# Summing the gated squares over the channels: GpSimd adds the two halves first, TensorE multiplies once a group

## The reference

```
zxbcdt = rmsnorm(x) @ Win                      # z, xBC, dt
xBC    = silu(causal_conv(xBC)); xh, Bm, Cm = split(xBC)
y      = ssd(xh, dt, A, Bm, Cm) + reversed ssd + D * xh
y      = y * silu(z)                           # the gated y, 128 channels a token
y      = y * rsqrt(mean(y * y, -1) + 1e-6) * gn_w
x      = x + y @ Wout
```

## Time and profile before

| | |
|---|---|
| time, median of 3 runs | 2498.42 us (2494.3 to 2499.23) |
| span of the profiled execution | 2496.4 us |
| PE busy | 1980.1 us, 79% |
| DVE busy | 1670.7 us, 67% |
| ACT busy | 1666.6 us, 67% |
| POOL busy | 1090.7 us, 44% |
| first `sum_squares` of a block to the last in the program | 941.4 to 2470.5 us |

### The profile page before, as it was taken

How to read it: one execution, slowest core, us unless ns; L and a number is a source line. 1 busy time by engine, 2 the same in 40 slices (tenths; PEclk the granted TensorE clock), 3 DMA queues, 4 the chain that set the end, 5 groups by cost and what they waited for, 6 DMA issues and landing times.

```text
span 2496.4 us, 58563 instructions
## 1 busy us (share of the span) xinstructions
PE 1980.1 (79%) x24262; PEld 1001.1 (40%) x24262; DVE 1670.7 (67%) x2423; ACT 1666.6 (67%) x2731; POOL 1090.7 (44%) x858
## 2 busy tenths in 40 slices
PE   4367677776777679979979979967997997996996
PEld 3122222222222235535525535534553552553553
DVE  3488888888888766556656656656655765665663
ACT  1276677676676657757857857866775775785784
POOL 0044444444444525516606625623551660662563
PEclk6578888888988889989989989988988998998997
DMA  4000000000000021022012111102102201211111
GB/s 159 0 0 1 1 0 0 1 1 0 1 1 0 0 65 38 18 65 49 19 56 47 30 55 39 39 18 62 41 14 66 49 18 56 47 30 42 40 39 35
DMA packets 95513, 77.46 MB, mean 31 GB/s; under 512 B 65936, under 2 KB 74128, under 8 KB 94736
## 3 DMA queue, kind: packets, MB, share of 16 engines
q1 hardware_dynamic: 91984, 73.32, 11.7%
q10 hardware_dynamic: 3264, 0.39, 0.1%
HBM read 27.02 MB, written 11.53 MB: 15 GB/s over the span
## 4 chain that ended last, share of the span: by engine, by line
PE 55%; DVE 20%; ACT 15%; issue 6%; POOL 2%; DMA 1%; ACTq 0%; POOLq 0%; SPq 0%; DVEq 0%
PE bank L593 10%; PE bank L662 7%; PE bank L625 6%; PE bank L674 6%; PE bank L606 5%; PE bank L682 5%; DVE Z L1271 4%; PE bank L521 3%; ACT bank L935 3%; PE bank L577 2%; ACT Z L827 2%; DVE XP L1337 2%; ACT SS L832 2%; DVE bank L1263 2%; POOL Y L986 2%
## 5 line engine op out<-in xcount | busy, mean ns | idle before, releaser
L986 POOL TENSOR_TENSOR Y<-Z 128x512 f32<-128x512 f32 x256 | 330.6, 1292 | 496.9 <-DVE Z L1271 320.4
L1018 POOL TENSOR_TENSOR SQ<-SQ,folded_weights 128x512 f32<-128x512 f32 x192 | 243.8, 1272 | 676.0 <-DVE SQ L1448 675.9
L1271 DVE TENSOR_TENSOR_SCAN Z<-SS,bank 128x512 f32<-128x512 f32 x256 | 309.9, 1211 | 0.5
L521 PE MATMUL bank<-Y,constants 128*128 128x512 f32 x512 | 298.0, 668 | 7.7 <-DVE bank L1279 7.6
L1024 POOL TENSOR_TENSOR SQ<-O,SQ 128x512 f32<-128x512 f32 x208 | 264.8, 1274 | 64.9 <-ACT O L931 36.5
L593 PE MATMUL bank<-folded_weights,work 128*64 128x128 f32 x4096 | 287.2, 285 | 0.0
L625 PE MATMUL bank<-SS,work 32*128 32x512 bf16 x1024 | 209.7, 389 | 63.0 <-ACT bank L935 45.0
L662 PE MATMUL bank<-SQ,work 128*32 128x64 f32 x8192 | 259.1, 227 | 0.6
L593 PEld LDWEIGHTS bank<-folded_weights,work 128*64 128x64 f32 x4096 | 225.9, 140 | 79.0 <-issue 79.0
L509 PE MATMUL bank<-work,Z 96*128 96x512 bf16 x256 | 113.8, 445 | 175.1 <-DVE Z L1271 175.0
L1390 DVE SCALAR_TENSOR_TENSOR work<-SQ,bank 64x512 f32<-64x512 f32 x256 | 175.5, 685 | 108.7 <-ACT SQ L903 106.6
(11 more groups left out here) (264 smaller groups left out, 3757.5 us busy)
## 6 DMA issues: line engine op xcount, KB each, us to landing
work<-XP SPq DMA_DIRECT2D x256, 134.0 KB, 2.4
decays_kept<-extra SPq DMA_DIRECT2D x24, 384.0 KB, 2.3
SS<-decays_kept SPq DMA_DIRECT2D x256, 24.0 KB
block_weights<-callw SPq DMA_DIRECT2D x8, 735.0 KB, 4.3
work<-decays_kept SPq DMA_DIRECT2D x240, 24.0 KB
Z<-state_sel SPq DMA_DIRECT2D x1, 2048.0 KB, 13.2
out<-O SPq DMA_DIRECT2D x2, 1024.0 KB, 8.5
constants<-consts SPq DMA_DIRECT2D x1, 1451.5 KB, 6.3
```

The source lines that it names most:

```text
L521: mm(bank[7], ident, hc[ta % 4], start=(ta % S1 == 0), stop=(ta % S1 == S1 - 1), skip_group_check=True).then_inc(sg("s1_acc"), 1)
L986: g.tensor_tensor(hc[t_ % 4], hs[t_ % 4], c_copy[t_ % 4], ALU.mult).then_inc(sg("s1_hc"), 1)
L1018: g.tensor_tensor(MM[u % 3], MM[u % 3], Dhalf, ALU.add).then_inc(sg("mixed"), 1)
L1271: v.tensor_tensor_scan(hs[t_ % 4], decay1[t_ % 2], bank[B_BANKS[t_ % 3]], 0.0, ALU.mult, ALU.add).then_inc(sg("s1_h"), 1)
```

## The change

GpSimd gets a step of its own in each group, `add_squares(k)`: it waits for the two squares of ACT and adds `squares[1]` onto `squares[0]`. PE's `sum_squares` waits for that step instead of for ACT, and does one matmul on `squares[0]` instead of two. Where the step stands in GpSimd's loop: before the mixing of u = 15, 23, ..., 63 for groups 0 to 6, and behind the loop for group 7.

```
                 def sum_squares(g):
-                    pe.wait_ge(sg("gated_squared"), c * 8 + g + 1)
+                    pe.wait_ge(sg("squares_added"), c * 8 + g + 1)
                     pe.wait_ge(sg("z_ready"), c * 16 + min(2 * g + 4, 16))
                     if g >= 1:
                         pe.wait_ge(sg("scaled"), c * 8 + g)
-                    for hd in range(2):
-                        last = mm(bank[sum_bank(g)], C("ssum"), squares[hd], start=(hd == 0), stop=(hd == 1))
-                    last.then_inc(sg("squares_psum"), 1)
+                    mm(bank[sum_bank(g)], C("ssum"), squares[0], start=True, stop=True).then_inc(sg("squares_psum"), 1)
...
+                def add_squares(k):
+                    pool.wait_ge(sg("gated_squared"), c * 8 + k + 1)
+                    g.tensor_tensor(squares[0], squares[0], squares[1], ALU.add).then_inc(sg("squares_added"), 1)
+
                 for u in range(L):
+                    if u >= 15 and (u - 15) % 8 == 0:
+                        add_squares((u - 15) // 8)
                     if u >= 20 and (u - 20) % 8 == 0:
                         grow((u - 20) // 8)
...
+                add_squares(7)
                 grow(6)
                 grow(7)
```

## The result

The changed kernel takes 2503.22 us (median of 20 runs, 2498.53 to 2506.06), the kernel before 2498.61 us in the 20 runs beside it. The ratio is 1.0015, with a 95% interval of 1.0009 to 1.0022: 3.7 us slower by the ratio, 4.6 by the medians. The forecast was 2502.4. In what follows the time of a variant is the median of its runs, to be held against 2498.61 and 2503.22; the ratio given with it is to other runs of the kernel before, made beside it. Of the 21 executions of the kernel before beside e1, e2, e3 and e5, 7 took 2515.9 to 2520.8 us at a lower granted clock, which puts the ratios of these four 0.1 to 0.3% too low, and one execution each of e7 (6014 us) and e8 (9277 us) is left out.

What follows compares the result with a forecast made beforehand. PE was taken to have the most work and over half the chain of waits; +2 (full-clock sums) - 7 (slow sums) + 9 (block ends) = +4 us on 2496.4 gave 2500.4 of span, median 2502.4, range 2488 to 2517.

Steps and rivals of the forecast that it cites:

- Part 1: At each sum on PE: one matmul less saves 0.86 us, 55 us over 64 sums if nothing else moved.
- Part 2: Between ACT's squares and PE's sum: GpSimd's addition makes the sum start 1.46 us after the squares, against 0.56.
- the forecast's +2: At 39 full-clock sums in groups 0 to 5: the wait fills the saved matmul, losing 0.04 to 0.05 us each.
- 9 slow places: Sums in groups 0 to 5 at 1.2 GHz: addition ready in time, matmul saved, -7 us, bounds -3 and -10.
- Part 3: GpSimd work behind the addition: free mid-block; at block ends y(63) starts 2.3 us late, +9 us over eight blocks.
- The cover of the mixing of u = 15 and 16: GpSimd mid-block: these mixings, delayed by the addition, still finish before PE needs them; 1.7 us of cover for u = 15.
- the middle of 0.6 and 1.7: Block ends: +1.1 us each, chosen between the clock rising just as long after dense work's start and rising later still.
- Part 4: GpSimd's 64 additions: 81 us on an engine 44% busy, mattering only through waits; DVE folding stays at 0.21 us by rows.
- rival 4: In 28 groups DVE folding delays GpSimd's addition by one instruction, 0.21 us: +6, 2508 us; chance 0.07.
- Rival 1: Waits before the sums pull PE's clock down in the groups: 13 more falls give +21, 2519 us; chance 0.17.
- Rivals 2 and 3: Block ends cheap, clock rising at its old moment: 2488, chance 0.12; reserve larger, PE not waiting: 2457, chance 0.06.

Runs made afterwards that it cites:

- e1: Changed kernel with the addition of group 6 moved behind the mixing of u = 63 instead of before it; 2486.61 us, ratio 0.9937 to the kernel before.
- e2: Changed kernel with PE making the sums of groups 0 to 5 one tau later (15 instead of 14); 2474.78 us, ratio 0.9884.
- e3: Kernel before with the second matmul of each sum left out and no addition, covering half the channels; 2458.96 us, ratio 0.9813.
- e5: Changed kernel with GpSimd's additions written to unused SBUF; PE waits for ACT and makes both matmuls; median 2528.4 us, ratio 1.007.
- e7: Kernel before with the sums of groups 0 to 5 one tau later, two matmuls, no addition; 2505.69 us, ratio 1.0041.
- e8: Changed kernel with every addition one place later, behind the mixing of u = 15, 23, ..., 63; 2486.71 us, ratio 0.9938.
- e4: Changed kernel with both matmuls kept in each sum, so PE waits for the addition without the saving; 2572.12 us, ratio 1.0284.

## Why the prediction was right

**Part 1, the matmul,** at 0.86 us: right. e3 takes 0.86 and e2 0.84 off a full-clock period, and e4 adds 0.87.

**Part 2, the handoff.** 1.46 us was stated and 1.40 measured (0.08 + 1.27 + 0.05; ACT to GpSimd was taken as 0.13, from a row in which GpSimd's idle time is put down to issue and not to ACT). With 1.06 for the sum a full-clock place comes to -0.01 and, by the period, -0.02 us and not +0.04: the forecast's +2 is -1. The extra 0.08 for a matmul that starts after a wait does not show in the time to the next one. For the 9 slow places -7 was forecast. The groups as a whole are -3.9, against -5 stated for both kinds together. A slow place gave its matmul back: from the squares to `y` it takes 4.2 and 4.4 us on average in the two executions of the kernel before and 3.3 to 3.4 in the three of the changed one. But their number, which the forecast left alone, went from 9 and 10 to 14, 14 and 10. With -1 for the full-clock places -3 is left for these, and the additional slow places are the likely reason that it is not -7.

**Part 3, the block end.** `y(63)` 2.2 us late (2.3 stated), +7.3 us in all (+9 stated, 0.9 a block instead of 1.1). e1 and e5 show that it is the place of the addition of group 6: taken out of the way it gives back 21.5 us of block ends, put there alone it costs 18.5. The cover of the mixing of u = 15 and 16 held (e5, e8). The rise of the clock came later, as assumed: in block 0 it is 2.8 us behind the start of the sum before and 4.5 behind it in the changed kernel. By how much was a choice, the middle of 0.6 and 1.7, and the 0.9 that came out lies nearer the lower; that the middle comes this near is in part luck.

**Part 4, the port.** By the rows alone the prediction left the folding at 0.21 us. That was wrong: the instruction takes 1.22, and folding instructions that take in one tensor only are longer too. The rule of the Trainium skill (SBUF — State Buffer, "Who interferes with whom") is what the traces of the changed kernel (1.22 us beside GpSimd) and of e8 (0.21 with GpSimd idle) agree with. The clause that it would not change the sum was right too, since the mixing of u = 16 has cover; rival 4, in which the addition is held up, did not happen: in the rows shown it starts 0.08 us after the squares, and the 1.40 us to the sum are the same in the groups with folding.

**The rivals.** Rival 1 (the clock) is part of the result and not the whole: slow time in the groups is 36 and 42 us before and 47 to 62 in the changed kernel, 16 more on average, which at half a us for each is a loss of 8 at the most, against the 21 of its first price. The Trainium skill (TensorE: Matmul & The Clock Gate, "A second HAM failure mode: psum-queue depth-cycling") has frequent short idle times swing the clock. Of that, e4's 78 us agree in direction, and the 45 of e2, without the wait; the 58 of e3, without it too, do not, so these runs leave it open. Rivals 2 and 3 did not happen.

**The sum** was +4; it is +3.4 by the parts, 3.7 by the ratio. The mechanism held in the groups and at the ends, but the closeness is in part luck: of the three terms +2, -7 and +9 the first came out 3 lower, the second 4 higher and the third 2 lower, and the rest of the span, which the sum took as fixed, scatters by 6 us.

## What to carry to other kernels

Before an operation is replaced by a cheaper one behind a handoff, measure the reserve between producer and consumer: here 0.56 us of reserve against 1.40 of handoff ate a saving of 0.86. Then place the new step: in a queue with work behind it, a step that waits belongs behind the instruction that another engine needs next (16.6 us here), and the consumer belongs late enough that it never waits (28.4 us here). Look at the end of a loop by itself; what has cover in the middle has none there.

## What the runs showed of the hardware

A DVE instruction with two SBUF inputs beside a GpSimd multiplication took 1.22 us instead of 0.21, up to 0.08 us behind the end of GpSimd's instruction. It is not only two inputs: a pair of folding instructions with one tensor input each, first in the kernel before and then in the changed one with GpSimd beside it,

```profile
1001.61 0.48 DVE L1101 TENSOR_SCALAR folded_weights<-block_weights 128x128 f32<-128x128 f32 x2
...
995.79 1.27 POOL L1013 TENSOR_TENSOR O<-O 128x512 f32<-128x512 f32 x1 [2.19 <-ACT O L956]
997.01 1.27 POOL L1028 TENSOR_TENSOR SQ<-SQ 128x512 f32<-128x512 f32 x1
...
996.62 1.75 DVE L1106 TENSOR_SCALAR folded_weights<-block_weights 128x128 f32<-128x128 f32 x2
```

takes 1.75 us instead of 0.48. Over the program DVE is busy for 46 us more; that time does no work and, here, costs none.

A slow clock costs less where the engine would have waited anyway: 0.7 to 1.0 us for most falls in the changed kernel, 1.5 to 1.6 for most in kernels in which PE had no wait at that place (before, e2, e3, e7). So a kernel with less PE work can give back part of its gain: e2 and e3 shortened the full-clock period by 0.84 and 0.86 us, 40 and 41 us over 48 groups, and the groups by 32; of e3's 44.7 us in groups and ends, another 8 went between the blocks and elsewhere outside them.
